# Magnitudes of the third score group on ScalarE and its causal mask on GpSimd, in the last twelve steps of an attention kernel

## The chip, the cores and the metric

The kernel runs on one core of a Trainium2 chip. The metric is the device time of one execution in microseconds (us). The engines are named as in the profile: PE is TensorE (matrix products), DVE is VectorE, ACT is ScalarE, POOL is GpSimd, SP is SyncE, which here only issues transfers.

## The reference, cut to what matters

The input x is 4 batches of 512 rows of 128. Three layers follow, each with its residual: a feed-forward part with top-1 routing over 8 experts, attention with 16 heads of 8 channels, and the feed-forward part again. Only the attention is touched:

```
L   = q k^T / sqrt(8)          L_y = q k_y^T / sqrt(8)
agg = sum_k exp(clip(L_y, -15, 15)) * mask + eps
w   = softplus(log(|L| + eps) - log(agg + eps)) * mask     # mask: k <= q
out = (w / (sum_k w + eps)) v
```

The softplus of a difference of logarithms is log(1 + |L| / agg). So the kernel scales q by 1 / agg, takes the magnitudes of the scores, and then the logarithm of 1 plus them. Where the magnitude is 0, the logarithm is 0, so the mask may be applied before the logarithm, or to its result.

## The kernel before, in words

Heads are handled two at a time, at partitions 0 and 64 of the products' rows, so there are 8 pairs of heads in each of 4 batches: 32 values of the number v (STEPS). The outer loop of each engine's program runs over s from 0 to 49. In step s the A part computes L_y of pair number s (for s < 32), its clip (DVE, line 1281) and exponentials with sums (ACT, line 944). The B part handles v = s - 12 (LAG is 12), for s from 12 to 43: scores L transposed, magnitudes, logarithms. From s = 32 on there is no A part; s = 32 to 43 are v = 20 to 31.

The B scores of one v are three fills of PSUM by PE (line 1649): group 0 is key tile 0 (512 queries), group 1 key tiles 3 and 1 (128 and 384), group 2 key tile 2 (256), each for both heads of the pair, so 1024, 1024 and 512 elements in each partition. There are three PSUM slots of two banks, filled in turn; a fill waits in slot_free until the fill three before it has been read. DVE's abs_scores (line 1296) reads each fill, takes the sign bit off with an integer and, with the causal mask in the same operand MB, and writes to one of three weight buffers in SBUF. ACT's logs (line 952) then takes the logarithm in place, in two instructions: part 0 is group 0 (1024), part 1 is groups 1 and 2 together (1536).

With the logarithms of an even and the following odd v, PE multiplies them by the values (weigh, line 1667) in four pieces by key tile, in the order 0, 1, 3, 2. For the pair (v, v + 1) with v even, pieces 0 and 1 stand in step v + 14, pieces 2 and 3 in step v + 15. Piece 3 is key tile 2, which is group 2 of the scores. ACT copies the sums out of PSUM (av_out, line 969), PE turns them (weighed_t, line 1680) into the free half of the slot of group 2, and DVE copies them out (heads_out, line 1308). In steps above 32, ACT's order in a step is: av_out (odd v), second logarithm of v - 1, first logarithm of v, then other work.

Once in every batch there is other work: POOL forms the factor for q from agg (agg_sums, line 679; scale_q, lines 685 and 690), PE turns the scaled q (line 1723), DVE casts it and takes the remainder (scaled_q_terms, lines 1330 and 1333), POOL makes the second and third bf16 term (its own scaled_q_terms, lines 737 and 739), SP writes the terms to the stacked operand (line 463), for which PE waits in step 12 + 8 b. For b = 3, scale_q stands in step 32 of POOL's program, scaled_q_terms and query_part (lines 695 to 702, a chain of ten small operations) in step 33, and PE's wait in step 36. normalise (lines 752 to 755) and value_sums (lines 714 and 716) follow in steps 37 and 38. DVE has the prefix of values, reciprocals, the residual and the moments of a batch.

Each engine carries out its own program in order; semaphores join them. s_read counts DVE's reads of fills, s_pb the scores, s_ln the logarithms, s_av the pieces.

Of the kernel before, what the change touches and what calls it, by code (L numbers as in the profile page):

```python
# [21 lines left out]
P = 128  # L22
NT = 16
NB, TB = 4, 4
# [22 lines left out]
STEPS = NB * HP  # L47
LAG = HP + 4
SEG_J = ((0,), (3, 1), (2,))
SEG_N = (512, 512, 256)  # L50
# [9 lines left out]
SLOTS = (slice(0, 2), slice(2, 4), slice(4, 6))  # L60
TWO_SLOTS = LAG
# [4 lines left out]
J_OFF = {0: 0, 3: 512, 1: 640, 2: 1024}  # L66
HEAD_W = 1280
# [11 lines left out]
END_STEP = (NB - 1) * HP + X_AT + 2  # L79
# [30 lines left out]
def leaving(v):  # L110

    return v - 3 if v % 2 == 1 and 0 <= v - 3 < STEPS else None


def fills_before(s):

    return 3 * min(s, STEPS) + 3 * max(0, min(s - LAG, STEPS))
# [7 lines left out]
def b_fill(v, g):  # L125

    return fills_before(v + LAG) + (2 * g if v + LAG < STEPS else g)


def slot(n):  # L130

    return n % 2 if n < 3 * TWO_SLOTS else (n + 2) % 3
# [8 lines left out]
HEADS_IN = {ao_fill(v): leaving(v) + 2 for v in range(STEPS + 3) if leaving(v) is not None}  # L141


def build(nc, x_in, wattn_in, wg_in, w1_in, w2_in, b2_in, out):
    f32, bf16, u32, i32 = mybir.dt.float32, mybir.dt.bfloat16, mybir.dt.uint32, mybir.dt.int32
    ALU, ACT, AX = mybir.AluOpType, mybir.ActivationFunctionType, mybir.AxisListType.X
    ds = bass.ds
    ctx = ExitStack()
    with ctx:
# [3 lines left out]
        def sem(name):  # L153
            return ctx.enter_context(nc.semaphore(name))
# [112 lines left out]
        PS = ctx.enter_context(nc.psum_tensor("PS", [P, 8, 512], f32))  # L267
# [72 lines left out]
        s_qps = sem("scaled_q_stacked")  # L340
        s_pb = sem("l_ready")
        s_read = sem("score_slots_read")
        s_ln = sem("ln_done")
        s_av = sem("av_done")
        s_aot = sem("av_out_of_psum")
        s_aotp = sem("av_transposed")
        s_ao = sem("av_copied")
# [23 lines left out]
        def weights(v):  # L371

            return (WB[:, 0].rearrange("p (r n) -> p r n", r=2), WB[:, 1].rearrange("p (r n) -> p r n", r=2),
                    R2W)[v % 3]
# [134 lines left out]
        def _(pool):  # L509
# [4 lines left out]
                               base=0, pattern=[[-1, P]], channel_multiplier=1).then_inc(s_c, 1)  # L514
# [6 lines left out]
                               base=0, pattern=[[1, P]], channel_multiplier=-1).then_inc(s_c, 1)  # L521
# [219 lines left out]
            def normalise(b):  # L741
# [5 lines left out]
                if b == NB - 1:  # L747
# [7 lines left out]
                pool.tensor_tensor(numf, numf, spread(den.rearrange("p (n o) -> p n o", o=1), 2, HD),  # L755
                                   ALU.mult).then_inc(s_num, 1)

            for s in range(END_STEP):
                for b in range(NB):
                    at = s - b * HP  # L760
                    if at == A_AT:
                        agg_sums(b)
                    if at == R_AT:
                        scale_q(b)
                    if at == Q_AT:
                        scaled_q_terms(b)
                    if at == C_AT - 5:
                        value_sums(b)
                    if at == V_AT:
                        key_counts(b)  # L770
                    if at == N_AT:
                        normalise(b)

                m = s - 1 + FIRST_PROJECTIONS
                if s == 1:
                    second_term(2)
                    third_term(2)
                if 0 < s < A_AT:
                    second_term(m)
                    third_term(m)  # L780
                elif s == A_AT:
                    second_term(m)
                elif s == R_AT:
                    third_term(m - 1)
                    second_term(m)
                elif s == Q_AT:
                    third_term(m - 1)
                    second_term(m)
                    third_term(m)
                for b in range(NB):  # L790
                    if s - b * HP == Q_AT:
                        query_part(b)
# [9 lines left out]
        def _(act):  # L802
# [144 lines left out]

            def logs(v, part):

                act.wait_ge(s_read, b_fill(v, (0, 2)[part]) + 1)  # L950
                w = weights(v)[:, :, (0, SEQ)[part]:(SEQ, HEAD_W)[part]]
                act.activation(w, w, ACT.Ln, bias=1.0, scale=1.0).then_inc(s_ln, 1)  # L952

            def scaled_q(b):

# [4 lines left out]
            def av_out(v):  # L960

                act.wait_ge(s_av, TB * (v // 2 + 1))
                if v == 0:

                    act.wait_ge(s_stk[7], STACK_DMAS)
                else:

                    act.wait_ge(s_aotp, v // 2)
                act.activation(AOT, PS[:, AV_BANK, :], ACT.Copy).then_inc(s_aot, 1)  # L969

            for s in range(END_STEP):
                v = s - LAG
                if s > STEPS and leaving(v) is not None:
                    av_out(leaving(v))
                if 1 <= v <= STEPS:
                    logs(v - 1, 1)
                if s <= STEPS and leaving(v) is not None:
                    av_out(leaving(v))
                if LAG <= s <= STEPS:
                    exponentials(s - 1, 2)  # L980
                if 0 <= v < STEPS:
                    logs(v, 0)
                for b in MIDDLE:
                    if s - b * HP == Q_AT + 1:
                        scaled_q(b)
                if s < STEPS:
                    exponentials(s, 0)
                    exponentials(s, 1)
                if s < LAG - 1:
                    exponentials(s, 2)  # L990
                after(s)
                for b in range(2):
                    if s == TURN_AT[b]:
                        copy_xnt(2, b, b + 1, XNT1)
                if s == TURN_AT[2] + 1:
                    copy_xnt(2, 2, 3, XNT1)
                if s == LN_EARLY:
                    deviations(4)
                if s == LN_EARLY + 1:
                    normal_rows(0, 6, 3)  # L1000
# [8 lines left out]
        def _(dve):  # L1009
# [291 lines left out]
            def heads_out(v):  # L1301

                dve.wait_ge(s_aotp, v // 2 + 1)
                w = 2 * (HD + 1)
                bank = 2 * slot(ao_fill(v + 3))
                for par in range(2):
                    at = v % HP * (HD + 1) + par * HP * (HD + 1)
                    dve.tensor_copy(
                        AO.rearrange("p i h c -> p i (h c)")[:, :, at:at + w],
                        PS[:, bank, AO_COL:AO_COL + TB * 2 * w].rearrange("p (i r) -> p i r", i=TB)  # L1310
                        [:, :, par * w:(par + 1) * w]).then_inc(s_ao, 1)
# [88 lines left out]
            for s in range(END_STEP):  # L1400
                v = s - LAG
                if v == 1:

                    dve.wait_ge(s_lo, 12)
                for g in range(3):
                    if 0 <= v < STEPS:
                        abs_scores(v, g)
                    if g == 2 and leaving(v) is not None:
                        heads_out(leaving(v))
                    if s < STEPS:  # L1410
                        clip_scores(s, g)
                    between(s, g)
                after(s)
                if s == LN_EARLY - 1:
                    variance(4)
                if s == LN_EARLY:
                    inverse(4)
                    route_scores(1, 0)
# [10 lines left out]
        def _(pe):  # L1429
# [187 lines left out]
            def slot_free(n):  # L1617

                if n == 3 * TWO_SLOTS:
                    pe.wait_ge(s_hi, 12)  # L1620
                    pe.wait_ge(s_rem, 12)
                elif n >= 2:
                    pe.wait_ge(s_read, n - (1 if n < 3 * TWO_SLOTS else 2))
                    if n - 3 in HEADS_IN:

                        pe.wait_ge(s_ao, HEADS_IN[n - 3])
# [29 lines left out]
            def weigh(v, piece):  # L1656

                j = WEIGH_TILES[piece]
                pe.wait_ge(s_ln, 2 * v + (3 if piece == 0 else 4))
                if piece == 0 and v:  # L1660
                    pe.wait_ge(s_aot, v // 2)
                b = v // HP
                for u in (v, v + 1):
                    for par in range(2):
                        quad = QUAD * (2 * par + u % 2)
                        head = ((b * TB + j) * H + par * HP + u % HP) * (HD + 1)
                        last = pe.matmul(PS[quad:quad + QUAD, AV_BANK, j * P:SEQ],  # L1667
                                         VF[:, head:head + QUAD],
                                         weights(u)[:, par, J_OFF[j]:J_OFF[j] + SEQ - j * P],
                                         start=piece == 0, stop=piece == TB - 1)  # L1670
                last.then_inc(s_av, 1)
# [68 lines left out]
            for s in range(END_STEP):  # L1740
# [51 lines left out]
                    turn(2, 2)  # L1792

                if s == LN_EARLY - 1:
                    pe.wait_ge(s_read, fills_before(END_STEP))
                    gate(1, 0, 0, 2)
                if s == LN_EARLY:
                    gate(1, 0, 2, 8)
# [58 lines left out]
```

## Time and profile before

| | us |
|---|---|
| median of 3 runs | 416.27 |
| lowest and highest run | 414.98, 416.46 |
| span of the profiled execution | 421.1 |
| its own time | not listed apart from the span |
| PE, DVE, ACT, POOL busy | 330.0, 304.9, 297.8, 149.6 |
| mean granted clock of PE | 0.868 |

The busy times are of one profiled execution, whose span is 4.8 us above the median of the runs. In the rows, a line begins with the start and the length of a group of instructions in us; the arrow in square brackets says how long the engine stood before it and what ended the wait. Neighbouring instructions of an engine overlap a little, so the next one starts before the length of the one before has passed. PEclk is the granted clock as a share of 2.4 GHz. The attention's last twelve steps lie between about 284.5 and 334 us.

### The profile page before, as it was taken

How to read it: one execution, taken by the hardware profiler on the slowest of the kernel's cores; microseconds unless marked ns; L12 is line 12 of the kernel's file. 1: busy time of each engine (PE TensorE's matmuls, PEld its weight loads, DVE VectorE, ACT ScalarE, POOL GpSimd, SP SyncE). 2: the span in 40 equal slices, each digit the busy share in tenths (PEclk: the TensorE clock that was granted, in tenths of full speed). 3: DMA queues.
4: the chain of work that ended last, by engine and by line, in shares of the span. 5: the costliest groups of instructions: out<-in, count | busy, mean ns of one | idle time of the engine just before them, and what ended most of it. 6: DMA issues, size and time to landing. Idle time of an engine off the chain costs nothing.

```text
span 421.1 us, 8327 instructions
## 1 busy us (share of the span) xinstructions
PE 330.0 (78%) x2412; PEld 195.9 (47%) x2412; DVE 304.9 (72%) x628; ACT 297.8 (71%) x866; POOL 149.6 (36%) x252
## 2 busy tenths in 40 slices
PE   6878899995766435778788677777978996889992
PEld 6638899752233111222334223242333473589992
DVE  5653443378899969999999999988999657444431
ACT  2915456424999979999999989996777646345561
POOL 5575544400443560021411214112530016654452
PEclk9989999996699655876958969878998989899997
DMA  8775666134478996001200012000300274666540
GB/s 248 263 222 153 199 162 173 46 107 138 133 203 224 220 243 134 0 2 38 64 0 2 0 39 63 2 2 0 101 0 2 66 264 121 189 189 180 166 134 26
DMA packets 37993, 47.61 MB, mean 113 GB/s; under 512 B 4288, under 2 KB 26816, under 8 KB 37696
## 3 DMA queue, kind: packets, MB, share of 16 engines
q1 hardware_dynamic: 33616, 36.20, 31.7%
q0 software_dynamic: 2560, 6.30, 5.3%
q10 hardware_dynamic: 1776, 4.60, 3.3%
q8 instruction: 21, 0.34, 0.3%
q14 instruction: 20, 0.16, 0.1%
HBM read 24.02 MB, written 6.29 MB: 72 GB/s over the span
## 4 chain that ended last, share of the span: by engine, by line
ACT 34%; PE 33%; DVE 13%; issue 6%; DMA 4%; POOL 3%; SPq 2%; DVEq 1%; another core or an unknown queue 1%; ACTq 1%; POOLq 0%
ACT R L944 14%; PE PS L1522 9%; ACT R L952 9%; PE PS L1532 8%; ACT CL L944 7%; PE PS L1667 3%; PE PS L1451 3%; PE PS L1475 2%; SPq L463 2%; DVE R L1296 2%; DVE R L1281 2%; DMA QPS<-R 2%; PE PS L1649 2%; DVE R L1027 1%; ACT R L969 1%
## 5 line engine op out<-in xcount | busy, mean ns | idle before, releaser
L1296 DVE TENSOR_TENSOR R<-PS,MB 128x1024 int32<-128x1024 int32 (+1 forms) x96 | 97.9, 1034 | 13.3 <-PE PS L1649 13.1
L836 ACT ACTIVATE R<-PS,R 128x128 f32<-128x128 f32 x184 | 52.6, 368 | 49.1 <-PE PS L1522 23.8
L952 ACT ACTIVATE R<-R 128x1024 f32<-128x1024 f32 x64 | 80.0, 1261 | 9.7 <-DVE R L1296 9.6
L944 ACT ACTIVATE R<-R 128x384 f32<-128x384 f32 (+2 forms) x192 | 77.1, 411 | 3.1 <-DVE R L1281 3.1
L1634 PE MATMUL PS<-R 64*128 64x512 bf16 (+3 forms) x256 | 40.1, 367 | 33.7 <-DVE CL L1281 16.3
L1281 DVE SCALAR_TENSOR_TENSOR R<-PS,MA 128x1024 f32<-128x1024 f32 x64 | 59.5, 946 | 1.1 <-PE PS L1634 1.1
L1667 PE MATMUL PS<-R,V 128*32 128x256 f32 (+3 forms) x512 | 56.3, 526 | 3.6 <-ACT R L952 3.5
L1522 PE MATMUL PS<-R 128*128 (+1 forms) x368 | 51.7, 283 | 6.2 <-DVE R L1162 4.5
L1649 PE MATMUL PS<-QPS,R 64*128 64x512 bf16 (+3 forms) x256 | 38.2, 349 | 15.5 <-DVE R L1281 8.4
L1522 PEld LDWEIGHTS PS<-R 128*128 128x128 f32 x368 | 44.6, 191 | 10.2 <-issue 8.5
L1532 PE MATMUL PS<-R 128*128 (+1 forms) x368 | 48.8, 276 | 0.7 <-ACT R L836 0.7
L1532 PEld LDWEIGHTS PS<-R 128*128 128x128 f32 x368 | 44.7, 192 | 1.1 <-ACT R L836 1.1
L1281 DVE SCALAR_TENSOR_TENSOR CL<-PS,MA 128x1024 f32<-128x1024 f32 x32 | 38.9, 1214 | 4.3 <-PE PS L1634 3.8
L944 ACT ACTIVATE CL<-CL 128x512 f32<-128x512 f32 x64 | 39.6, 625 | 1.6 <-DVE CL L1281 1.5
L1634 PEld LDWEIGHTS PS<-R 64*128 64x128 bf16 x256 | 12.1, 103 | 59.6 <-DVE R L1296 25.2
L1649 PEld LDWEIGHTS PS<-QPS,R 64*128 64x128 bf16 x256 | 10.2, 98 | 62.3 <-DVE R L1296 23.8
L636 POOL DMA_INDIRECT R<-rows_d,R x32 | 31.4, 983 | 21.5 <-PE PS L1522 7.9
L944 ACT ACTIVATION_READ_ACCUMULATOR R<-R 128x1 f32 x192 | 37.8, 197 | 0.0
L1181 DVE SCALAR_TENSOR_TENSOR R<-R,scoef (+1 forms) x46 | 16.3, 354 | 28.2 <-DVE R L1187 23.4
L1475 PE MATMUL PS<-onesb 128*128 128x512 bf16 x120 | 33.2, 435 | 0.0
L1187 DVE SCALAR_TENSOR_TENSOR R<-PS,scoef,R 128x128 f32 (+1 forms) x46 | 16.1, 350 | 23.4 <-PE PS L1532 19.2
L1680 PE MATMUL PS<-ident,R 128*128 128x36 f32 x128 | 18.5, 293 | 8.3 <-ACT R L969 5.2
(184 smaller groups left out, 460.8 us busy)
## 6 DMA issues: line engine op xcount, KB each, us to landing
R<-w SPq DMA_DIRECT2D x38, 258.0 KB
R<-R SPq DMA_DIRECT2D x32, 128.0 KB, 2.4
R<-R SPq DMA_DIRECT2D x16, 256.0 KB, 7.9
QPS<-R SPq DMA_DIRECT2D x32, 128.0 KB, 2.4
R<-w ACTq DMA_DIRECT2D x8, 258.0 KB
rows_d<-X SPq DMA_DIRECT2D x8, 256.0 KB, 3.9
R<-w ACTq DMA_DIRECT2D x1, 2048.0 KB, 8.3
rows_d<-R SPq DMA_DIRECT2D x8, 256.0 KB, 2.4
```

The source lines that it names most:

```text
L636: pool.indirect_dma_start(XS[:, t, :], None, rows_d, bass.IndirectOffsetOnAxis(source[:, t:t + 1], 0))\
L836: last = act.activation(HT[:, k % 2, c * P:(c + 1) * P], PS[:, k % 2, c * P:(c + 1) * P], ACT.Gelu, bias=W1[:, k, F + c:F + c + 1])
L944: act.activation(e, e, ACT.Exp, scale=SCALE, accum_out=aggf[:, ds(s + (2 * i + par) * STEPS, 1)])\
L952: act.activation(w, w, ACT.Ln, bias=1.0, scale=1.0).then_inc(s_ln, 1)
L1281: dve.scalar_tensor_tensor(out=CL[g][:, :, :], in0=PS[:, SLOTS[slot(a_fill(s, g))], 0:n], scalar=-CLIP, in1=spread(mask, 1, 2), op0=ALU.ma ...
L1296: dve.tensor_tensor(weights(v)[:, :, at:at + n].bitcast(i32), PS[:, SLOTS[slot(b_fill(v, g))], 0:n].bitcast(i32), spread(mask, 1, 2), ALU. ...
L1475: pe.matmul(PS[:, bank, :], onesb[:, :], spread(onesb[:, :].rearrange("p (o n) -> p o n", o=1), 1, TB), start=True, stop=True)
L1522: last = pe.matmul(PS[:, s % 2, c * P:(c + 1) * P], W1[:, s % RING, c * P:(c + 1) * P], XT[:, ds(e * (-P) + P * s, P)], start=True, stop=True)
L1532: last = pe.matmul(PS[:, 6 + s % 2, 0:P], HT[:, s % 2, c * P:(c + 1) * P], W2[:, ds(e * F + c * P, P)], start=c == 0, stop=c == FC - 1)
L1634: last = pe.matmul(PS[:, SLOTS[slot(n)], :][:, par, at:at + (i + 1) * P], QS[rows, hp, (b * TB + i) * P:(b * TB + i + 1) * P], YS[rows, hp ...
L1649: last = pe.matmul(PS[:, SLOTS[slot(n)], :][:, par, at:at + w], KS[rows, hp, (b * TB + j) * P:(b * TB + j + 1) * P], QPS[rows, (b + 1) % 2 ...
L1667: last = pe.matmul(PS[quad:quad + QUAD, AV_BANK, j * P:SEQ], VF[:, head:head + QUAD], weights(u)[:, par, J_OFF[j]:J_OFF[j] + SEQ - j * P], ...
```

## The change

For v >= 20 (ABS_FROM = STEPS - LAG), group 2's magnitudes are taken by ACT with an Abs out of PSUM (magnitudes(v)), in step v + 13, ahead of the second logarithm of the same v. This writes no mask. DVE's abs_scores leaves out group 2 there. POOL sets the part of the diagonal tile above the diagonal to 0 after the logarithm (lower_triangle(v), an affine select over 2 x 128 elements), at the head of its step v + 13. PE's piece of key tile 2 waits for POOL's masks of both v's; slot_free waits for ACT's magnitudes where the fill was a group 2; dve_reads(n) is the number of reads that DVE has made by fill n. heads_out waits for group 2's scores, for which it stood behind DVE's own read before.

```diff
+ABS_FROM = STEPS - LAG
+FULL_FILLS = fills_before(STEPS)
+
+
+def dve_reads(n):
+
+    k = n - FULL_FILLS
+    return n + 1 if k < 0 else FULL_FILLS + 2 * (k // 3) + min(k % 3, 1) + 1
...
+            def lower_triangle(v):
+
+                pool.wait_ge(s_ln, 2 * v + 2)
+                diagonal = weights(v)[:, :, J_OFF[2]:J_OFF[2] + P]
+                pool.affine_select(out=diagonal, in_=diagonal, compare_op=ALU.is_ge, fill=0.0, base=0,
+                                   pattern=[[0, 2], [1, P]], channel_multiplier=-1).then_inc(s_low, 1)
+
             for s in range(END_STEP):
+                if ABS_FROM < s - LAG <= STEPS:
+                    lower_triangle(s - LAG - 1)
...
             def logs(v, part):
 
-                act.wait_ge(s_read, b_fill(v, (0, 2)[part]) + 1)
+                if v >= ABS_FROM and part == 1:
+                    act.wait_ge(s_read, dve_reads(b_fill(v, 1)))
+                    act.wait_ge(s_abs, v - ABS_FROM + 1)
+                else:
+                    act.wait_ge(s_read, dve_reads(b_fill(v, (0, 2)[part])))
...
+            def magnitudes(v):
+
+                act.wait_ge(s_pb, 6 * v + 6)
+                act.wait_ge(s_av, TB * ((v - 3) // 2) + 4)
+                if b_fill(v, 2) in HEADS_IN:
+
+                    act.wait_ge(s_ao, HEADS_IN[b_fill(v, 2)])
+                act.activation(weights(v)[:, :, 1024:HEAD_W], PS[:, SLOTS[slot(b_fill(v, 2))], 0:SEG_N[2]],
+                               ACT.Abs).then_inc(s_abs, 1)
...
                 if s > STEPS and leaving(v) is not None:
                     av_out(leaving(v))
+                if ABS_FROM < v <= STEPS:
+                    magnitudes(v - 1)
                 if 1 <= v <= STEPS:
                     logs(v - 1, 1)
...
                 dve.wait_ge(s_aotp, v // 2 + 1)
+                if ABS_FROM <= v + 3 < STEPS:
+
+                    dve.wait_ge(s_pb, 6 * (v + 3) + 6)
...
                 for g in range(3):
-                    if 0 <= v < STEPS:
+                    if 0 <= v < STEPS and (g < 2 or v < ABS_FROM):
                         abs_scores(v, g)
...
                 elif n >= 2:
-                    pe.wait_ge(s_read, n - (1 if n < 3 * TWO_SLOTS else 2))
+                    before = n - (2 if n < 3 * TWO_SLOTS else 3)
+                    if before >= FULL_FILLS and (before - FULL_FILLS) % 3 == 2:
+                        pe.wait_ge(s_abs, (before - FULL_FILLS) // 3 + 1)
+                    else:
+                        pe.wait_ge(s_read, dve_reads(before))
...
                 pe.wait_ge(s_ln, 2 * v + (3 if piece == 0 else 4))
+                if j == 2 and v >= ABS_FROM:
+                    pe.wait_ge(s_low, v - ABS_FROM + 2)
...
                 if s == LN_EARLY - 1:
-                    pe.wait_ge(s_read, fills_before(END_STEP))
+                    pe.wait_ge(s_read, dve_reads(fills_before(END_STEP) - 2))
+                    pe.wait_ge(s_abs, LAG)
```

## Rows read from the trace of the kernel before

**Rows 1.** Stretches: length, busy us (count) of PE, PEld, DVE, ACT, POOL; PEclk, DMA share, GB/s.
```profile
284.50:302.00 17.50, 14.97 (x122) 5.89 (x120) 15.55 (x26) 11.27 (x14) 7.76 (x19) 0.85 0.22 60
302.00:334.00 32.00, 27.94 (x258) 12.66 (x262) 28.06 (x45) 23.29 (x23) 5.08 (x10) 0.95 0.01 1
293.60:296.00 2.40, 2.29 (x14) 0.44 (x14) 2.37 (x7) 1.54 (x2) 0.04 (x1) 0.50 0.00 0
302.00:309.00 7.00, 5.63 (x60) 2.26 (x60) 6.96 (x10) 5.38 (x5) 1.00 (x3) 1.00 0.01 2
```

**Rows 2.** Groups, 284.5 to 334 us: busy us, mean ns | idle before, by releaser.
```profile
L1296 DVE TENSOR_TENSOR R<-PS,MB 128x1024 int32<-128x1024 int32 x24 | 28.7, 1214 | 4.9 <-PE PS L1649 4.8
L952 ACT ACTIVATE R<-R 128x1536 f32<-128x1536 f32 x12 | 17.7, 1478 | 2.2 <-DVE R L1296 2.2
L952 ACT ACTIVATE R<-R 128x1024 f32<-128x1024 f32 x12 | 12.6, 1053 | 4.3 <-DVE R L1296 4.3
...
L1296 DVE TENSOR_TENSOR R<-PS,MB 128x512 int32<-128x512 int32 x12 | 8.2, 682 | 1.8 <-PE PS L1649 1.8
```

**Rows 3.** Waits, 284.5 to 334 us: us in total, times, longest.
```profile
ACT R L952 <- DVE R L1296: 6.5, 8, 1.7
```

**Rows 4.** PE in order of time, 291 to 309.5 us.
```profile
293.71 1.94 PE L1667 MATMUL PS<-R,V 128*32 128x512 f32 x8 [0.69 <-ACT R L952]
...
297.54 0.86 PE L1667 MATMUL PS<-R,V 128*32 128x128 f32 x16
298.33 1.13 PE L1695 MATMUL PS<-V,tri 128*128 128x512 f32 x2
...
302.10 0.39 PE L1649 MATMUL PS<-QPS,R 64*128 64x512 bf16 x2 [0.43 <-DMA QPS<-R]
302.42 1.06 PE L1667 MATMUL PS<-R,V 128*32 128x512 f32 x8
...
304.00 0.85 PE L1667 MATMUL PS<-R,V 128*32 128x384 f32 x8
304.78 0.39 PE L1649 MATMUL PS<-QPS,R 64*128 64x512 bf16 x2
...
308.99 1.07 PE L1667 MATMUL PS<-R,V 128*32 128x512 f32 x8 [0.80 <-ACT R L952]
```

**Rows 5.** DVE in order of time, 286 to 303 us.
```profile
291.37 2.92 DVE L1296 TENSOR_TENSOR R<-PS,MB 128x1024 int32<-128x1024 int32 x3
...
294.49 0.68 DVE L1330 CAST R<-PS 128x512 bf16<-128x512 f32 x1
295.20 0.69 DVE L1333 TENSOR_TENSOR R<-PS,R 128x512 f32<-128x512 f32 x1
```

**Rows 6.** POOL in order of time, 286 to 303 us.
```profile
295.96 0.61 POOL L737 CAST R<-R 128x512 bf16<-128x512 f32 x1 [4.13 <-DVE R L1333]
...
297.90 0.37 POOL L695 TENSOR_SCALAR rt<-rt 128x64 f32<-128x64 f32 x1
...
302.06 0.37 POOL L702 TENSOR_SCALAR ck<-rt 128x64 f32<-128x64 f32 x1
```

**Rows 7.** POOL's affine selects by shape, whole span: busy us, mean ns | idle.
```profile
L548 POOL TENSOR_SCALAR_AFFINE_SELECT MA<-MA 128x128 f32<-128x128 f32 x2 | 0.5, 292 | 0.0
...
L532 POOL TENSOR_SCALAR_AFFINE_SELECT bound<-bound 128x184 f32<-128x184 f32 x1 | 0.5, 508 | 0.1
```

**Rows 8.** ACT in order of time, 272 to 370 us.
```profile
306.02 0.60 ACT L969 ACTIVATE R<-PS 128x512 f32<-128x512 f32 x1 [1.10 <-PE PS L1667]
306.52 2.42 ACT L952 ACTIVATE R<-R 128x1536 f32<-128x1536 f32 x2
...
338.46 1.28 ACT L812 ACT_TABLE_LOAD   x1
```

**Rows 9.** PE in order of time, 309 to 336 us.
```profile
324.91 1.93 PE L1667 MATMUL PS<-R,V 128*32 128x512 f32 x8 [0.53 <-ACT R L952]
...
333.79 1.06 PE L1667 MATMUL PS<-R,V 128*32 128x512 f32 x8
```

More of the change, by code:

```diff
@@ L342, in build @@
         s_read = sem("score_slots_read")
+        s_abs = sem("magnitudes_of_act_ready")
+        s_low = sem("magnitudes_masked")
         s_ln = sem("ln_done")
```

## The prediction

> **What bounds the kernel now.** The change touches twelve of the attention's fifty steps, so I read that stage only, in this order: busy time by stretch, the groups of instructions in it, who waits for whom, and then the order of time of each engine around every new wait. A step here is one turn of the outer loop, s; it handles the scores of pair number v = s - 12. The twelve steps are s = 32 to 43 (v = 20 to 31) and lie between 284.5 and 334 us.
>
> The stage has no single bound [rows 1]. From 302 to 334 us, 32 us, PE is busy 27.9, DVE 28.1, ACT 23.3 and POOL 5.1. DVE's share is twenty-four 128x1024 masks of magnitudes at 1.21 us and twelve 128x512 ones at 0.68; ACT's is twelve logarithms of 1536 at 1.48 and twelve of 1024 at 1.05 [rows 2]. ACT waited 6.5 us for DVE in eight waits [rows 3]. So both ACT and PE stand in line behind DVE some of the time, and DVE behind PE: a loop through three engines, in which work taken off DVE counts only where DVE is what ends a wait.
>
> **Name of the loop.** I call the four groups of products of a pair of v's w0, w1, w2, w3, in the order that PE issues them. w0 and w1 stand in an even step, w2 and w3 in the next. w0 waits for the odd v's first logarithm, w1 for its second. After w3 ACT copies the sums out (line 969), PE turns them (line 1680), and ACT does the next two logarithms, which free the next w0.
>
> **Part 1, DVE is relieved.** Twelve masks of 512 leave DVE. Two successive ones or what follows start about 0.58 to 0.60 after each other (0.68 less the overlap of neighbours: the three masks of 291.37 take 2.92 in all, 2 x 1.13 + 0.66 [rows 5]). 12 x 0.60 = 7.2 us of DVE's time. On the path, at most the waits of ACT for DVE, 6.5 us [rows 3].
>
> Before s = 36 the relief has one clear effect: two masks fewer stand ahead of the cast at 294.49 that begins the last scaled-query terms, so this cast and the remainder behind it (295.20) come 2 x 0.59 = 1.18 us earlier [rows 5]. The transfers that follow end later than PE needs them by only 0.43 us, the wait at 302.10 [rows 4]; that is all there is to gain there, 0 to 0.43.
>
> **Part 2, the mask moves to POOL, and POOL works in its own order.** lower_triangle(v) stands at the head of POOL's step v + 13, and w3 of a pair waits for both of its masks. For the first pair, w3(20, 21) stands in PE's step 35, and needs lower_triangle(21), in POOL's step 34. Ahead of it in POOL's step 33 are scaled_q_terms(3) and query_part(3). Before, these run from 295.96 to 302.43 (the last instruction starts at 302.06 and takes 0.37) [rows 6], and the first waits for DVE's remainder of 295.20, which takes 0.69 [rows 5]. With the remainder 1.18 earlier, POOL is through at 302.43 - 1.18 = 301.25.
>
> The price of the mask itself no row shows in its shape, 2 x 128. Of this form 128 elements took 0.29 and 184 took 0.51 [rows 7]. I take 0.6, from 0.5 to 0.75. With 0.08 to begin it is done at about 301.95.
>
> PE wants w3 at about 297.9 (w2 and w3 together start at 297.54 and the next instruction 0.79 later [rows 4]). PE works in order, so it stands for 4.05 us. Behind w3 are, in step 35, the value prefix, the second and third score fills and the turning of the sums, and then the fill of step 36. Before, from 297.9 to the end of that work took 302.10 - 0.43 - 297.9 = 3.77 us, without a wait [rows 4]. After: 301.95 + 3.77 = 305.7 against 302.10, that is **+3.6 us**. Nothing hides it: all later work of PE and ACT follows from this fill. DVE's lead gives nothing back, since PE fills its slots.
>
> **Part 3, the clock after the stall.** Where PE had waited (0.69 before 293.71, and more ahead of it) the granted clock of the next stretch was 0.50, the 1.2 GHz level, and w0 took 1.94 us; with the clock at 1.00 it took 1.06 [rows 1, 4]. A stall of 4 us is far longer than any wait in this stage. If all of the 3.77 us behind it ran at the lower level, it would take up to 3.4 us more; if none, 0. A third to a half of it is my value, **+1.4 us**. The Trainium skill ("TensorE: Matmul & The Clock Gate", section "Part 1: The HAM clock gate (the "warmup" mystery)") says that the default is the throttled state and that activity releases it, so that PE starts slow after a pause; by that alone the sum would take the upper part of 0 to 3.4, and the trace agrees in direction.
>
> **Part 4, ACT takes work into the loop.** A magnitude of 512 out of PSUM has as its nearest row the copy of 512 out of PSUM: 0.60, the next instruction 0.50 later [rows 8]. The second logarithm now waits on ACT's own magnitudes, so it can't overlap them: 0.60 + 0.05 = 0.65 before it starts. Queued behind that wait are both logarithms and the next copy out, and PE's turning of the sums now waits for the magnitudes too, 0.5 later than before.
>
> The loop before, from the fill at 302.10 to w0 at 308.99, is 6.89 us [rows 4]. After: the second logarithm begins 0.05 + 0.65 after the third fill, takes 1.48 and frees w1 at 2.2; w1 0.78 (304.00 to 304.78); fill 0.32; w2 and w3 0.79; copy out 0.05 + 0.50; magnitudes 0.65; logarithms 1.38 and 1.05; 0.05 to w0. Sum 7.77, **+0.9 us** for the first pair. POOL's masks lie beside this (each has w1, a fill and w2 as cover, some 1.4 us against 0.7).
>
> From w0 at 308.99 to the last at 333.79 are three pairs in 24.80 us, 8.27 each [rows 4, 9]: already above 7.77, because other work (residual, moments, turns, prefix) stood in the way. What of it stood on DVE is now beside the path; what stood on PE or ACT remains. So each pair grows by between 0 and 0.9; near 0.2, **+0.5 us** for three. The last pair: magnitudes instead of the mask ahead of the last logarithm, 0.65 against 0.68 [rows 2, 8]: 0.
>
> PE now idles about 2 of 7.8 us in each pair. At 324.91 a w0 already ran at the lower level with 1.93 [rows 9]. More such stretches: **+0.4 us**, from 0 to 2.5.
>
> One condition that no row shows is that Abs needs no other table. The Trainium skill ("ScalarE: Activation LUTs", section "Table sets: the hidden batching unit") says that abs is in every set, so this costs nothing; no run here shows it yet.
>
> **Sum.** 3.6 + 1.4 + 0.9 + 0.5 + 0.4 - 0 = **+6.8 us**. What follows the stage (the second feed-forward part) starts later and is otherwise the same. The profiled execution's span is 421.1, 4.8 above the median of the runs, 416.27; no separate time of it is listed. Against its own span the forecast is 427.9; the differences come from instructions that both executions have, so I put them on the median: 416.3 + 6.8 = 423.1 us.
>
> **Rivals.**
> 1. No stall in POOL's order, only the loop through ACT: for it, if PE comes to w3 late or query_part ends early. Against: 4.05 us have to vanish, and the rows leave no gap on POOL. 416.3 + 0.9 + 0.5 + 0.4 = 418.1. Chance 0.12.
> 2. DVE was the bound and ACT had the room, the other side: from s = 32 on, each pair gets shorter by two masks of 0.60 where DVE ended the wait. For it: the 6.5 us of ACT's waits [rows 3]. Against: ACT gets back 7.2 to 7.8 us of work in the same order in which it waited, and w0 waits for ACT. It decides if the stall at w3 is under about 2 us. Two thirds of 6.5 less 1.8: -2.5, 413.8. Chance 0.06.
> 3. The stall and the low clock in full: most of the 3.4 us, and low stretches in two more pairs, +2: 416.3 + 3.6 + 3.4 + 0.9 + 0.5 + 2 = 426.7. Chance 0.14.
> 4. Abs and Ln each reload a table in every step, 24 loads of 1.28 [rows 8] = 30.7 us on ACT: 416.3 + 30.7 = 447. Nothing in the copies between logarithms speaks for it [rows 8]. Chance 0.02.
> The forecast (stall and part of the clock) has 0.66.
>
> **How the numbers follow.** A measurement tells about 0.5%, 2.1 us, from no change. Slower by more: the forecast, 3, 4 and a little under half of 1: 0.66 + 0.14 + 0.02 + 0.04 = 0.86. Within: the rest of 1 and a part of 2: 0.09. Faster: 0.05. The range leaves out some of 1 and 2 below and the top of 3 above: 418.3 to 426.8.
>
> **What would show it.** Right: in PE's order of time a wait of about 4 us ahead of one L1667 group in step 35, released by POOL's new affine select, the latter directly behind line 702's instruction; the cast at 294.49 about 1.2 earlier; a granted clock at the lower level after the stall; ACT's magnitudes about 0.60, and w0 to w0 at 7.8 us or more with waits for ACT. Wrong: no PE wait over 1 us for POOL, masks far from 0.6 us, or pairs that get shorter than 6.9 us.

## The result and the profile after

The changed kernel takes 425.34 us (median of 6 runs, 424.22 to 427.43) against 415.84 (6 runs): 1.0237 times the time before, with a 95% interval from 1.0204 to 1.0269, and 9.5 us slower by the medians. Forecast were 423.1, in a range from 418.3 to 426.8.

The spans of the two profiled executions differ by only 1.8 us, 421.1 and 422.9. The profiled execution of before was a slow one, outside the stage that was changed: a run's time is its span and 1.9 us here (422.9 goes with 424.81), so it stands for 423.0, 7 us above the median, and what follows the stage took it 85.5 us, against 81.9 after and 80.5 to 82.4 in the seven traces of the experiments on chips 9 and 14. I therefore measure the stage inside each trace, from w0 of step 32 to the last w1. Before, this is 284.60 to 335.60, 51.0 us; after, 281.24 to 341.04, **59.8 us**. These 8.8 us are nearly all of the 9.5. Before the stage the profile of before is 3.4 us later, and behind it 3.6 us longer, and that is the gap between the two ways to count. The 51.0 rests on this one trace; the stages of three kernels that were traced twice moved by 0.6 to 1.4 us between their traces.

The table has the distance from each w0 to the next, named by the even v of its pair, in us. The forecast column adds the terms of the prediction to the distances of before.

| | before | forecast | after |
|---|---|---|---|
| w0(18) to w0(22) | 17.82 | 22.8 | 22.72 |
| w0(22) to w0(24) | 6.57 | 7.5 | 8.40 |
| w0(24) to w0(30), three pairs | 24.80 | 25.7 | 26.35 |
| w0(30) to the last w1 | 1.81 | 1.8 | 2.33 |
| stage | 51.0 | 57.8 | 59.8 |

DVE in order of time, kernel after (start, length, then what the engine did; in brackets the idle time ahead and what ended it), and behind it POOL in the same way:

```profile
290.62 0.69 DVE L1373 TENSOR_TENSOR R<-PS,R 128x512 f32<-128x512 f32 x1
```
```profile
287.86 0.41 POOL L774 TENSOR_SCALAR_AFFINE_SELECT R<-R 128x256 f32<-128x256 f32 x1
291.38 0.61 POOL L749 CAST R<-R 128x512 bf16<-128x512 f32 x1 [3.11 <-DVE R L1373]
292.08 1.16 POOL L751 TENSOR_TENSOR R<-R 128x512 bf16<-128x512 f32 x1
293.33 0.37 POOL L707 TENSOR_SCALAR rt<-rt 128x64 f32<-128x64 f32 x1
...
297.50 0.37 POOL L714 TENSOR_SCALAR ck<-rt 128x64 f32<-128x64 f32 x1
297.82 0.41 POOL L774 TENSOR_SCALAR_AFFINE_SELECT R<-R 128x256 f32<-128x256 f32 x1
301.96 0.41 POOL L774 TENSOR_SCALAR_AFFINE_SELECT R<-R 128x256 f32<-128x256 f32 x1 [3.73 <-ACT R L977]
```

The first line is DVE's remainder, on which POOL's chain waits; it answers to [rows 5], POOL's lines to [rows 6]. The first mask has passed by 288.3. The second (297.82) stands directly behind the chain of ten small operations. PE in order of time over the same stretch answers to [rows 4]:

```profile
289.73 1.94 PE L1713 MATMUL PS<-R,V 128*32 128x512 f32 x8 [0.47 <-ACT R L977]
...
294.33 0.66 PE L1713 MATMUL PS<-R,V 128*32 128x128 f32 x8
298.38 0.81 PE L1713 MATMUL PS<-R,V 128*32 128x256 f32 x8 [3.39 <-POOL R L774]
299.12 2.08 PE L1741 MATMUL PS<-V,tri 128*128 128x512 f32 x2
...
303.54 0.50 PE L1693 MATMUL PS<-QPS,R 64*128 64x256 bf16 x4
303.96 1.06 PE L1713 MATMUL PS<-R,V 128*32 128x512 f32 x8
...
306.67 0.85 PE L1713 MATMUL PS<-R,V 128*32 128x384 f32 x8 [1.20 <-ACT R L977]
...
309.93 1.05 PE L1726 MATMUL PS<-ident,R 128*128 128x36 f32 x8 [0.97 <-ACT R L986]
...
312.36 1.93 PE L1713 MATMUL PS<-R,V 128*32 128x512 f32 x8 [0.95 <-ACT R L977]
```

The reader sees w2 at 294.33 and w3 only at 298.38, released by POOL's mask; the prefix product behind it takes 2.08 us and not 1.13; and in the next pair three waits for ACT: 1.20 before w1, 0.97 before the sums are turned, 0.95 before w0. The granted clock (PEclk, third from the right) shows why the prefix product is slow. The columns are those of [rows 1]:

```profile
289.73:303.96 14.23, 10.84 (x62) 3.65 (x62) 6.27 (x9) 6.66 (x7) 6.23 (x15) 0.68 0.27 74
303.96:341.04 37.08, 30.11 (x262) 12.80 (x261) 24.31 (x39) 29.66 (x34) 7.27 (x15) 0.91 0.05 14
299.10:302.10 3.00, 3.00 (x11) 1.07 (x9) 0.29 (x1) 2.78 (x4) 0.14 (x1) 0.50 0.00 0
```

ACT in order of time, kernel after, the pair behind the stall (L1004 is the copy of the sums, L986 the magnitudes, L977 the logarithms); it answers to [rows 8]:

```profile
304.44 0.60 ACT L986 ACTIVATE R<-PS 128x512 f32<-128x512 f32 x1 [1.60 <-DVE R L1348]
305.13 2.43 ACT L977 ACTIVATE R<-R 128x1536 f32<-128x1536 f32 x2
308.70 0.60 ACT L1004 ACTIVATE R<-PS 128x512 f32<-128x512 f32 x1 [1.13 <-PE PS L1713]
309.19 0.59 ACT L986 ACTIVATE R<-PS 128x512 f32<-128x512 f32 x1
309.87 2.43 ACT L977 ACTIVATE R<-R 128x1536 f32<-128x1536 f32 x2
```

And the groups and waits of the stage after, 281.2 to 341 us (busy us, mean ns | idle before), against [rows 2] and [rows 3]:

```profile
L977 ACT ACTIVATE R<-R 128x1024 f32<-128x1024 f32 x12 | 12.5, 1045 | 1.0 <-DVE R L1333 1.0
L986 ACT ACTIVATE R<-PS 128x512 f32<-128x512 f32 x12 | 7.1, 590 | 2.2 <-DVE R L1348 2.2
```
```profile
DVE R L1333 <- PE PS L1693: 16.5, 12, 6.1
...
PE PS L1726 <- ACT R L986: 3.9, 4, 1.0
...
PE PS L1713 <- ACT R L977: 3.4, 6, 1.2
PE PS L1713 <- POOL R L774: 3.4, 1, 3.4
...
ACT R L986 <- DVE R L1348: 2.2, 3, 1.6
...
ACT R L977 <- DVE R L1333: 1.0, 2, 0.8
```

ACT's logarithms waited 6.5 us for DVE before (7.5 counted up to the last w1) and 1.0 after: the relief is real, though the magnitudes now wait 2.2 us for DVE. But DVE's masks now wait 16.5 us for PE (6.5 before), and ACT's own magnitudes are what PE waits for before it turns the sums.

### The profile page after: what moved, and what is told of

It is laid out like the page before. It is cut to its first block, busy times and chain, and to the rows that moved or that the text cites. A ratio compares the mean times of both kernels' runs of the same rounds, so it can differ in the third digit from the quotient of the medians.

```text
span 422.9 us, 8364 instructions
## 1 busy us (share of the span) xinstructions
PE 334.9 (79%) x2412; PEld 198.1 (47%) x2412; DVE 298.3 (71%) x616; ACT 304.7 (72%) x878; POOL 155.2 (37%) x264
## 4 chain that ended last, share of the span: by engine, by line
PE 39%; ACT 29%; DVE 12%; issue 7%; DMA 5%; POOL 4%; SPq 1%; ACTq 1%; POOLq 0%; DVEq 0%
ACT R L965 11%; PE PS L1562 11%; ACT R L977 9%; PE PS L1572 9%; ACT CL L965 5%; PE PS L1713 5%; DVE R L1318 3%; PE PS L1491 3%; DMA R<-rows_d,R 2%; PE PS L1693 2%; DVE CL L1318 2%; DVE R L1333 2%; PE PS L1482 1%; SPq L475 1%; DVE R L1064 1%
## 5 line engine op out<-in xcount | busy, mean ns | idle before, releaser
L1333 DVE TENSOR_TENSOR R<-PS,MB 128x1024 int32<-128x1024 int32 (+1 forms) x84 | 90.8, 1087 | 21.3 <-PE PS L1693 21.2
L977 ACT ACTIVATE R<-R 128x1024 f32<-128x1024 f32 x64 | 79.8, 1261 | 2.5 <-DVE R L1333 1.3
L1713 PE MATMUL PS<-R,V 128*32 128x256 f32 (+3 forms) x512 | 58.8, 545 | 9.1 <-ACT R L977 5.6
L1693 PE MATMUL PS<-QPS,R 64*128 64x512 bf16 (+3 forms) x256 | 39.4, 361 | 12.7 <-DVE R L1318 7.6
L1693 PEld LDWEIGHTS PS<-QPS,R 64*128 64x128 bf16 x256 | 10.3, 99 | 61.4 <-issue 22.8
L1726 PE MATMUL PS<-ident,R 128*128 128x36 f32 x128 | 19.5, 304 | 10.6 <-ACT R L1004 4.3
```

The costliest lines, as they stand in the source:

```text
L1333: dve.tensor_tensor(weights(v)[:, :, at:at + n].bitcast(i32), PS[:, SLOTS[slot(b_fill(v, g))], 0:n].bitcast(i32), spread(mask, 1, 2), ALU. ...
L1693: last = pe.matmul(PS[:, SLOTS[slot(n)], :][:, par, at:at + w], KS[rows, hp, (b * TB + j) * P:(b * TB + j + 1) * P], QPS[rows, (b + 1) % 2 ...
L1713: last = pe.matmul(PS[quad:quad + QUAD, AV_BANK, j * P:SEQ], VF[:, head:head + QUAD], weights(u)[:, par, J_OFF[j]:J_OFF[j] + SEQ - j * P], ...
```

## The experiments

Two theories stood against each other. **Order**: most of the loss is PE standing for one mask that comes late in POOL's program, and the low clock behind it. **Load**: the loss is ACT's new work in the loop, and the stall only takes up time that would have been lost anyway. The stage of each kernel, read in its trace as above, stands beside its ratio to the kernel before on the same chip (the chips differ, so ratios are compared, not times).

**e1_order**, one mask moved ahead of query_part:

```diff
-                if ABS_FROM < s - LAG <= STEPS:
+                if ABS_FROM < s - LAG <= STEPS and s != STEPS + 2:
                     lower_triangle(s - LAG - 1)
...
                     if s - b * HP == Q_AT:
+                        if s == STEPS + 1:
+                            lower_triangle(ABS_FROM + 1)
                         query_part(b)
```

> The changed kernel with one mask moved: POOL's lower_triangle(21) stands ahead of query_part(3) in step 33 and no longer behind it. My theory (about 5 us of the 9.5 are PE standing at piece 3 of the first pair for this mask and the low clock behind it, about 4 are ACT's magnitudes in the loop): no wait of PE for POOL over 0.5 us, the stage shorter by 4.5 to 5, a time of 420.0 to 421.0, so 4 to 5 above the kernel before. Rival (the stall only uses time that PE would have spent waiting for the last stack of scaled q or for ACT, and the loop through ACT is all of the loss): 424.5 or more, as the changed kernel.

Measured: 417.14 us, ratio 1.0041 (0.9999 to 1.0083); stage 53.6 us. PE's wait for POOL is gone: POOL's mask stands between the third term and the small operations (order of time of POOL), and w3 follows w2 at once (PE, w2 and w3 as one group):

```profile
296.09 0.61 POOL L749 CAST R<-R 128x512 bf16<-128x512 f32 x1 [2.56 <-DVE R L1375]
297.90 0.41 POOL L774 TENSOR_SCALAR_AFFINE_SELECT R<-R 128x256 f32<-128x256 f32 x1
298.40 0.37 POOL L707 TENSOR_SCALAR rt<-rt 128x64 f32<-128x64 f32 x1
```
```profile
298.14 0.96 PE L1715 MATMUL PS<-R,V 128*32 128x128 f32 x16
```

One instruction's place was worth 6.2 us of the 8.8 in the stage. The theory of load is out as the whole cause; my own number for the gain, 4.5 to 5, was too low. The traced execution took 422.10 us, 5.0 above the median of this kernel, so the stage was read again in a second trace, below: 54.2.

**e2_pool_alone**, the kernel before with lower_triangle and PE's wait for it, everything else as before:

```diff
...
             for s in range(END_STEP):
+                if ABS_FROM < s - LAG <= STEPS:
+                    lower_triangle(s - LAG - 1)
...
                 pe.wait_ge(s_ln, 2 * v + (3 if piece == 0 else 4))
+                if j == 2 and v >= ABS_FROM:
+                    pe.wait_ge(s_low, v - ABS_FROM + 2)
```

> The kernel before with POOL's masks and PE's waits for them added, and DVE's masks of all three groups kept (POOL masks what is masked already). My theory: query_part ends at about 302.4 on the clock of the profile before, since DVE isn't relieved, the mask at 302.8; PE stands 4.9 us at piece 3 of the first pair, 0.4 of it was a wait before, and 1 to 1.5 us of low clock follow: 421.0 to 422.0, 5.5 above the kernel before. Rival (the magnitudes on ACT are the loss): within 1 us of the kernel before, 416 to 417.

Measured: 421.13 us, ratio 1.0113 (1.0040 to 1.0185); stage 58.6 us. PE's row, kernel e2_pool_alone:

```profile
300.11 1.08 PE L1682 MATMUL PS<-R,V 128*32 128x256 f32 x8 [4.69 <-POOL R L766]
301.12 2.08 PE L1710 MATMUL PS<-V,tri 128*128 128x512 f32 x2
```

The wait is 4.69, as expected (4.9), and longer than in the changed kernel, since DVE isn't relieved and POOL's chain starts later. With no added work on ACT the stage is 7.6 us longer than before. The times show less: 5.7 us by the medians, 4.7 by the ratio (four runs). With the 2.8 of e3_no_mask, below, the stage would be 10.4 us longer; with both halves it was 8.8 in the first trace and 10.2 in the repeat.

**e3_no_mask**, the changed kernel without lower_triangle and its wait, so the magnitudes on ACT alone.

```diff
-                if ABS_FROM < s - LAG <= STEPS:
-                    lower_triangle(s - LAG - 1)
...
-                if j == 2 and v >= ABS_FROM:
-                    pe.wait_ge(s_low, v - ABS_FROM + 2)
```

> The changed kernel without POOL's masks and PE's waits for them; the diagonal tile of the third group stays unmasked in the last twelve pairs, which leaves a part of the computation out. It is the magnitudes on ACT alone. My theory: 420.0 to 421.0, the same as with the order mended to within 0.5, since eleven of the twelve masks have cover. Rival 1 (the twelve masks cost each a little): 1 us or more under the kernel with the order mended. Rival 2 (the magnitudes on ACT cost nothing, all of it is POOL): 416 or less.

Measured: 418.33 us, ratio 1.0046 (1.0007 to 1.0086); stage 53.8 us. That is e1_order within its spread (1.0041; 53.6): with the order mended, the twelve masks of POOL cost nothing that can be measured, and the rest of the loss comes with the magnitudes on ACT. The absolute time is 2 us below what I expected. PE's w0(24) stood for ACT as in the changed kernel, but ran at the full clock:

```profile
309.31 1.06 PE L1709 MATMUL PS<-R,V 128*32 128x512 f32 x8 [0.95 <-ACT R L975]
```

**e4_busy_wait**, twelve idle products on PE while it waits for the mask:

```diff
+                if j == 2 and v == ABS_FROM:
+                    pe.wait_ge(s_qrem, NB)
+                    idle_products(12, 7)
                 if j == 2 and v >= ABS_FROM:
                     pe.wait_ge(s_low, v - ABS_FROM + 2)
```

> The changed kernel with twelve idle products of 512 columns on PE in a free bank ahead of piece 3 of the first pair, so that PE is busy while it waits for the mask. The products take 2.6 us at the full clock and 5.1 at the low one; the wait is 3.4. My theory (1.4 us of the loss are the low clock behind the stall): a granted clock of 1.00 behind the mask, the prefix product back from 2.1 to 1.1 us, 1 to 1.5 us under the changed kernel, 424. Rival (the clock behind the stall costs nothing, since PE waits later anyway): the same as the changed kernel, 425.3.

Measured: 423.02 us, ratio 1.0145 (1.0066 to 1.0224); stage 57.8 us, 2.0 under the changed kernel. PE in order of time, and the busy time and clock behind the mask (columns as in [rows 1]):

```profile
297.13 2.76 PE L1515 MATMUL PS<-onesb 128*128 128x512 bf16 x12
301.22 0.64 PE L1716 MATMUL PS<-R,V 128*32 128x256 f32 x8 [1.33 <-POOL R L774]
301.79 1.13 PE L1744 MATMUL PS<-V,tri 128*128 128x512 f32 x2
```
```profile
301.20:304.00 2.80, 2.78 (x20) 1.35 (x20) 0.69 (x1) 1.98 (x3) 0.00 (x0) 1.00 0.00 0
```

The mask comes no sooner, but w3 takes 0.64 and not 0.81, the prefix product 1.13 and not 2.08. By the traces the low clock behind the stall was worth 1.3 us to the next w0 (22.72 to 21.41) and 0.7 in later pairs. By the times alone the difference to the changed kernel is not certain: the intervals overlap, and 2.0 us of stage is little more than the 1.4 by which two traces of the changed kernel differ.

**What is left on ACT.** Three kernels, all with the order of e1_order, move what stands around the magnitudes. e6_mag_first:

```diff
-                if s > STEPS and leaving(v) is not None:
-                    av_out(leaving(v))
                 if ABS_FROM < v <= STEPS:
                     magnitudes(v - 1)
+                if s > STEPS and leaving(v) is not None:
+                    av_out(leaving(v))
```

> The mended order, and in ACT's odd steps the magnitudes of v - 1 ahead of the copy of the sums out of PSUM, no longer behind it. In the kernel with the order mended ACT stands 1.13 us before that copy in most pairs. My theory (what is left of the loss, 2.6 us of stage, comes from where the magnitudes stand in ACT's order): they fill that idle time, PE's wait before it turns the sums falls from 0.97 to about 0.39 us, 0.5 us per pair in four or five pairs: the stage from w0 of step 32 to the last w1 51.0 to 51.8 us and not 53.6, a time of 415 to 416. Rival (ACT has too much work, in whatever order: 0.65 us more in each step): no change, 53.6 and 417.

Measured: 421.80 us beside 421.83 of the kernel before on this chip, ratio 0.9998 (0.9966 to 1.0030); stage 52.2 us. PE's wait before it turns the sums:

```profile
307.65 1.08 PE L1728 MATMUL PS<-ident,R 128*128 128x36 f32 x8 [0.39 <-ACT R L1006]
```

0.39, where it was 0.97: the same magnitudes, a place earlier, stand in time in which ACT waited for w3. The stage is 0.4 us longer than I expected at most; the time, relative to the kernel before, is as expected.

e8_heads_after turns the wait between the two readers of one PSUM bank round:

```diff
                 act.wait_ge(s_av, TB * ((v - 3) // 2) + 4)
-                if b_fill(v, 2) in HEADS_IN:
-
-                    act.wait_ge(s_ao, HEADS_IN[b_fill(v, 2)])
...
                 dve.wait_ge(s_aotp, v // 2 + 1)
                 if ABS_FROM <= v + 3 < STEPS:
 
-                    dve.wait_ge(s_pb, 6 * (v + 3) + 6)
+                    dve.wait_ge(s_abs, v + 3 - ABS_FROM + 1)
```

> The mended order, and the wait between the two readers of the third group's bank turned round: DVE's heads_out waits for ACT's magnitudes of the odd v, where ACT waited for heads_out. My theory: w1 comes 0.3 to 0.45 us earlier in each pair (PE waited 0.9 to 1.1 us for it), the stage 51.8 to 52.5, a time of 415.5 to 416.5. Rival (DVE, now later with the first magnitudes of the next v, holds up the first logarithm and so the third): no gain, or up to 1 us more than 53.6.

Measured: 425.11 us beside 421.83, ratio 1.0064 (1.0025 to 1.0104); stage 53.2 us. The last w1 waits 0.94 and not 1.26, and w0(22) to w0(24) takes 7.75 and not 8.08, as in e1_order, but DVE now stands up to 2.62 us for ACT:

```profile
313.41 0.37 DVE L1347 COPY R<-PS 128x72 f32<-128x72 f32 x2 [2.25 <-ACT R L985]
...
322.67 0.37 DVE L1347 COPY R<-PS 128x72 f32<-128x72 f32 x2 [2.62 <-ACT R L985]
```

My expectation missed: alone it gains nothing that can be measured. Taking the wait away without another in its place was not tried, since then nothing would order the two readers of the bank.

e9_both has both edits.

> The mended order with both of these. If the two delays stand one behind the other in the loop, as I think, the gains add: stage 49.8 to 50.8, time 414 to 415.3, at or just under the kernel before. If ACT's total work is the bound, it stays at 53 or above and 416.5 to 417.

Measured: 421.77 us beside 421.83, ratio 0.9983 (0.9942 to 1.0024); stage 51.2 us. The stage is 2.4 us shorter than in e1_order, where the edits alone brought 1.4 and 0.4; 49.8 to 50.8 were expected. The times don't tell it from e6_mag_first, so that the gains add is not shown by them.

**e10_even**, only even v on ACT and POOL, their magnitudes ahead of the copy of the sums (counts of reads follow):

```diff
+def on_act(v):
+
+    return v >= ABS_FROM and v % 2 == 0
...
-                if ABS_FROM < s - LAG <= STEPS:
+                if on_act(s - LAG - 1) and s - LAG <= STEPS:
                     lower_triangle(s - LAG - 1)
...
-                    if 0 <= v < STEPS and (g < 2 or v < ABS_FROM):
+                    if 0 <= v < STEPS and (g < 2 or not on_act(v)):
                         abs_scores(v, g)
...
-                    pe.wait_ge(s_low, v - ABS_FROM + 2)
+                    pe.wait_ge(s_low, (v - ABS_FROM) // 2 + 1)
```

> Only every second third group (even v) goes to ACT and POOL, with its magnitudes ahead of the copy of the sums, in ACT's idle time; odd v stay on DVE. No mask stands behind query_part for the first pair, w1 waits for no magnitudes of ACT, and DVE is relieved of 0.6 us a pair. My theory: no loss is left and some of DVE's waits go: stage 49.0 to 50.5 against 51.0 of the kernel before, time 413.5 to 415. Rival (DVE's time was worth nothing in this stage): 51.0, 415.4, the same as before.

Measured: 419.31 us beside 421.83, ratio 0.9931 (0.9895 to 0.9967); stage 50.0 us. The interval lies below 1, so it is faster than the kernel before, if only by 0.7%. The three pairs from w0(24) to w0(30) take 23.36 us, here and in the repeat below, against 24.80 before. The edit, which isn't shown whole, changes more than the load: for odd v, ACT's wait for heads_out goes too, and heads_out no longer waits for the scores itself. Which of these brings how much was not separated. ACT in order of time, kernel e10_even (L988 magnitudes, L1006 the copy, L982 logarithms):

```profile
306.26 0.58 ACT L988 ACTIVATE R<-PS 128x512 f32<-128x512 f32 x1
307.46 0.60 ACT L1006 ACTIVATE R<-PS 128x512 f32<-128x512 f32 x1 [0.61 <-PE PS L1712]
```

ACT has done the magnitudes and still waits 0.61 us for w3.

**The three that matter again**, side by side.

> The changed kernel again, beside the two that follow on one chip. 1.021 to 1.026 times the kernel before, as in the first measurement.

> The kernel with the order mended, again. By the stage in the traces (53.6 us against 51.0 and 59.8) it is 6.2 us faster than the changed kernel and 2.6 slower than the one before: 1.004 to 1.009. If it were 1.015 or more, the single trace would have flattered it.

> Only even v on ACT and POOL, again. By the stage in the trace (49.98 against 51.0) 1 us faster than the kernel before: 0.993 to 0.999. If the first ratio, 0.993, was luck, this one holds 1.

| | us | ratio to before | stage, first and again |
|---|---|---|---|
| changed | 425.35 | 1.0227 (1.0188 to 1.0265) | 59.8, 61.2 |
| order mended | 417.29 | 1.0047 (1.0016 to 1.0077) | 53.6, 54.2 |
| even v only | 413.95 | 0.9952 (0.9926 to 0.9978) | 50.0, 50.6 |
| before | 415.10 | | 51.0, the first trace alone |

The changed kernel's second trace has a wait of 4.49 us for the mask instead of 3.39:

```profile
300.55 1.08 PE L1713 MATMUL PS<-R,V 128*32 128x256 f32 x8 [4.49 <-POOL R L774]
```

PE came to it earlier (its w0, w1 and w2 ran at the full clock), and gained nothing by that. Behind the mask it lost more than in the first trace: all of the 7.44 us from w3 to the next w0, in which PE was busy throughout, have a granted clock of 0.50, and this w0 still ran at the lower level:

```profile
301.56 2.08 PE L1741 MATMUL PS<-V,tri 128*128 128x512 f32 x2
...
307.99 1.93 PE L1713 MATMUL PS<-R,V 128*32 128x512 f32 x8
```

## Why the prediction was right, and where its sizes were off

The stall in POOL's order, the low clock behind it and the longer loop through ACT are all in the trace. Of the added time 6.8 us were forecast and 9.5 measured. In the first trace 2.0 of the 2.7 that are missing lie in part 4; the other 0.7 lie outside the stage, and no run says where.

**Part 1** held. Anchored at w0(18), the cast comes 1.2 us earlier (289.91 in the trace, 284.60 - 281.24 = 3.36 to be added, against 294.49); forecast 1.18. ACT's logarithms had less to wait for DVE, 1.0 us after 6.5 [rows 3], which was worth little, since PE and ACT itself are what is late next.

**Part 2** held in mechanism and size. The mask took 0.41 us, below my 0.5 to 0.75 (the shape of 184 elements, 0.51 [rows 7], was a poor guide: 256 cost less). w3 started at 298.38, 301.74 on the clock of before, against 301.95 forecast. The wait itself was 3.39 us, not 4.05, since PE came to it later; in the second trace it was 4.49.

**Part 3** held in mechanism, and its size holds for one trace only. The level was the one that was named, 0.50 behind the stall. From the start of w3 to the next w0 were 4.36 us with PE kept at the full clock (e4_busy_wait), 5.58 in the changed kernel and 7.44 in its repeat, so the low clock cost 1.2 and 3.1 us there; forecast were 1.4, out of 0 to 3.4. Parts 2 and 3 together, w0(18) to w0(22), are 4.9 us more than before in the first trace (forecast 5.0) and 7.0 in the second (24.82 against 17.82). That the first agrees to 0.1 us is luck; why the clock came back sooner in one execution than in the other no run shows.

**Part 4** was mis-sized, and this is the step that failed in part. Forecast were 0.9 for the first pair, 0.9 for the three that follow (0.5 and 0.4 of clock) and 0 for the last; the trace has 1.8, 1.55 and 0.5. What I left out is the wait in magnitudes(v) on s_ao. For odd v the third group shares its bank with the turned sums, so the order is: scores, then DVE's heads_out, then ACT's magnitudes. I had counted from the scores straight to ACT. ACT's row at 304.44 shows it, with 1.60 of idle time that heads_out ended and not the fill, and DVE's row of heads_out:

```profile
303.96 0.37 DVE L1348 COPY R<-PS 128x72 f32<-128x72 f32 x2 [0.93 <-PE PS L1693]
```

The third fill ended at about 303.82 (0.28 of the 0.50 behind 303.54), so of the 1.60 us some 0.6 are this wait: the second logarithm began 1.31 us behind the fill, and 0.70 were forecast. The last w1 has it again: 2.33 us behind w0 against 1.81. Neither hangs on the stall: e1_order, e3_no_mask and r2_order all have 8.06 to 8.08 us for the first pair and 2.33 for the last w1, and e8_heads_after, without this wait, has 7.75 and 2.01. In the three pairs between, ACT's part was forecast well, and the clock was not: e3_no_mask and r2_order, with w0(24) at the full clock, took 25.06 and 25.09, 0.3 more than before (forecast 0.5), and the changed kernel, with w0(24) at the lower level, 26.35. That leaves some 1.3 us for the clock, where I had put 0.4. Not all pairs reached the 7.8 us that I had named as a sign: 26 to 28 took 7.57, against 7.45 before.

**How the parts divide** when each is undone by itself: order 6.2 to 7.0 us of the stage (changed against mended, both pairs of traces), 8.1 by the medians of the last three kernels; load on ACT 2.6 to 3.2 of the stage, 2.2 by the medians. So the stall was undersized (5.0) and the load close (1.8) by this count, and the other way round by the count inside the first trace. A likely cause, argued and not shown, is that the stall and the magnitudes together also bring low clock into the later pairs, which the count inside the trace puts down to the load: w0(24) took 1.56 to 1.94 us in all three traces that have both, and 1.06 or 1.07 in e1_order, e3_no_mask and r2_order. Whether a mended kernel also keeps a gain of DVE's relief ahead of w0(22) isn't shown: w0(18) to w0(22) is 17.14 us in the first trace of e1_order, but 18.71 in the repeat and 18.34 in e3_no_mask, and 17.82 before.

**The rivals.** Rival 1, no stall, is what e1_order makes true: 1.0041 and 1.0047, 1.7 to 2 us, where I had 1.8. Rival 2, DVE as the bound with room on ACT, fails for this kernel; for half of the change there was room: e10_even is 1.1 us faster by medians of 413.95 and 415.10. Rival 3, the low clock in full and low stretches in two more pairs, had 426.7, and the measured 425.34 lies nearer to it than to my 423.1. Its clock behind the stall is too dear for the first trace (1.2 of 3.4 us) and nearly right for the second (3.1); of the later w0, two ran at the lower level in the first trace (1.93, 1.93) and one did before (1.93). So the truth lies between the forecast and rival 3, and I gave the clock too little. Rival 4, a table load by Abs, is out: each of the twelve took 0.59 us among logarithms and no load stands in the stage. The Trainium skill ("ScalarE: Activation LUTs", section "Table sets: the hidden batching unit") says that abs is in every table set, and the trace agrees.

## What to carry to other kernels

Work that is moved to an idle engine runs at its place in that engine's program: look up what stands ahead of it there at the moment when its first user is ready, above all where a long chain of small operations does. POOL was busy 37% of the span and still made PE wait 3.4 to 4.5 us; moving one line got back 6.2 us of the 8.8 in the stage. When you count the wait of a moved operation, look at everything its own code waits for, also at a result of another engine that shares its bank. And of work given to an engine inside a loop of waits, try only as much as fits into its idle time ahead of what it waits for: half of the change, placed there, was a small gain (0.5 and 0.7%).

## What the runs showed of the hardware

An affine select of 2 x 128 float32 on POOL took 0.41 us, one of 128 took 0.29 and one of 184 in 23 rows of 8 took 0.51 [rows 7]: the shape counts, not only the number. ACT's Abs out of PSUM took 0.59 us for 512, as the copy does (0.60), and DVE's mask of 512 took 0.68. A logarithm that waits for the Abs started 0.68 to 0.69 us behind its start (304.44 to 305.13), 0.2 later than an instruction that needn't wait (308.70 to 309.19, 0.49).

The granted clock fell not only behind the long stall: ahead of 312.36 PE had stood for 0.97 and 0.95 us, and w0 took 1.93 us at the lower level. But the same two waits ahead of the same w0 left it at 1.06 or 1.07 us in e1_order, e3_no_mask and r2_order, so these waits alone don't decide it. And once low, the clock stayed low for different times under busy PE: it was back before the next w0 (1.06) in the first trace of the changed kernel, and had not come back 7.44 us behind the start of w3 in the second.
